# Early-fusion transformer block: rotated q and k summed in PSUM by identity products instead of on VectorE, and epsilons taken into the sums

## The reference

```
q, k = rmsnorm(q), rmsnorm(k)                    # over 16 channels, x * rsqrt(mean(x*x) + RMS_EPS)
rot(x) = concat(x1*c + x2*s, -x1*s + x2*c)       # q and k, 2 x 16 sub-heads, halves of 8
attn = softmax(causal(q k^T / sqrt(16)))         # 16 sub-heads
out = (attn[even] - lam * attn[odd]) @ v         # 8 heads, 32 wide
out = layernorm(out, eps 1e-5) * (1 - LAMBDA_INIT)
h = h + out @ Wproj^T
```

## Time and the profile before

| what | value |
| --- | --- |
| median of 3 runs | 659.81 us (658.97 to 660.0) |
| the profiled execution's own time | 662.52 us |
| its span, first to last instruction | 660.8 us |
| mean granted TensorE clock | 0.948 |
| TensorE matmuls busy | 576.4 us (87%) |
| VectorE busy | 554.1 us (84%) |
| ScalarE busy | 322.1 us (49%) |
| GpSimd busy | 309.8 us (47%) |

### The profile page before, as it was taken

How to read it: one execution, slowest core, us unless ns; L and a number is a source line. 1 busy time by engine, 2 the same in 40 slices (tenths; PEclk the granted TensorE clock), 3 DMA queues, 4 the chain that set the end, 5 groups by cost and what they waited for, 6 DMA issues and landing times. The chain is left out here.

```text
span 660.8 us, 14226 instructions
## 1 busy us (share of the span) xinstructions
PE 576.4 (87%) x3666; PEld 470.0 (71%) x3666; DVE 554.1 (84%) x1444; ACT 322.1 (49%) x760; POOL 309.8 (47%) x455
## 2 busy tenths in 40 slices
PE   5665568999999999999999998589999999999996
PEld 4554455767776776777677676478888888888885
DVE  5999847898889889888988985498888888888884
ACT  2242215655665665566565564244544444445442
POOL 2455523555455445545554553155455445545542
PEclk9878776999999999999999997789999999999999
DMA  6900000011111111111111101111111111111111
GB/s 173 325 17 23 24 16 18 27 38 41 30 40 35 35 35 38 40 34 37 35 41 29 42 23 46 30 39 49 48 54 52 54 48 54 49 48 48 57 32 35
DMA packets 33734, 31.99 MB, mean 48 GB/s; under 512 B 6098, under 2 KB 32050, under 8 KB 33714
## 3 DMA queue, kind: packets, MB, share of 16 engines
q1 hardware_dynamic: 33714, 31.75, 16.3%
HBM read 23.02 MB, written 8.71 MB: 48 GB/s over the span
## 5 line engine op out<-in xcount | busy, mean ns | idle before, releaser
L741 PE MATMUL bank<-v_sb,pt 113*113 113x33 f32 x1024 | 109.1, 262 | 0.0
L741 PEld LDWEIGHTS bank<-v_sb,pt 113*113 113x113 f32 x1024 | 108.4, 181 | 0.7 <-issue 0.7
L858 POOL TENSOR_SCALAR_AFFINE_SELECT pt<-pt 113x452 f32<-113x452 f32 x128 | 73.9, 600 | 68.5 <-ACT pt L798 68.5
L798 ACT ACTIVATE pt<-bank 113x452 f32<-113x452 f32 x128 | 63.1, 545 | 38.2 <-PE bank L729 38.2
L138 PE MATMUL bank<-wgu_hi,fx_hi 128*128 128x512 f32 x174 | 69.5, 399 | 8.0 <-DVE fx_lo L1131 8.0
L1177 POOL TENSOR_TENSOR h_deq<-fh,fhb 128x704 f32<-128x704 f32 x29 | 40.3, 1389 | 68.8 <-DVE fhb L1084 56.3
L729 PE MATMUL bank<-q_blk,k_t 64*113 64x452 f32 x256 | 67.7, 605 | 0.0
L138 PE MATMUL bank<-wgu_hi,fx_lo 128*128 128x512 f32 x174 | 66.8, 384 | 0.0
L138 PE MATMUL bank<-wgu_lo,fx_hi 128*128 128x512 f32 x174 | 66.7, 384 | 0.0
L138 PE MATMUL bank<-wqkv_hi,xo_hi 128*113 128x256 f32 (+1 forms) x128 | 50.3, 393 | 17.7 <-DVE xo_lo L923 17.7
L1191 POOL TENSOR_TENSOR fh<-fh,fhb 128x704 f32<-128x704 f32 x29 | 40.3, 1391 | 42.2 <-DVE fhb L1145 42.2
(11 more groups left out here) (160 smaller groups left out, 1531.3 us busy)
## 6 DMA issues: line engine op xcount, KB each, us to landing
xb<-h_dram SPq DMA_DIRECT2D x29, 129.0 KB, 2.1
rb<-h_dram SPq DMA_DIRECT2D x29, 128.0 KB, 2.0
h_dram<-h SPq DMA_DIRECT2D x32, 112.9 KB
out<-res SPq DMA_DIRECT2D x28, 128.0 KB, 1.7
px<-in_patches SPq DMA_DIRECT2D x9, 384.0 KB, 10.1
hx<-in_txt SPq DMA_DIRECT2D x32, 77.0 KB
hr<-in_txt SPq DMA_DIRECT2D x32, 77.0 KB
wf<-in_wgu SPq DMA_DIRECT2D x1, 1408.0 KB, 8.0
```

The source lines that it names most:

```text
L741: mm = pe.matmul(pv_ps[s % 2][0:T, s // 2, :], pt[0:T, s, :], v_sb[0:T, s // 2, :], start=True, stop=True, skip_group_check=True)
L798: act.activation(pt[0:T, GS * g:GS * (g + 1), :].rearrange("p s t -> p (s t)"), sc_ps[g % 2][0:T, :], ACT.Exp, scale=1.0 / math.sqrt(HD)). ...
L858: pool.affine_select(out=grp, in_=grp, compare_op=ALU.is_ge, fill=0.0, base=0, pattern=[[0, GS], [1, T]], channel_multiplier=-1).then_inc( ...
```

## The change

The VectorE instruction that adds the cosine and sine parts is gone, with its tile qkr. TensorE now makes the transposed sum: for each of the four chunks of 128 columns it multiplies the cosine part by the identity and then the sine part by the identity into the same PSUM block. These are ordinary float32 products and no transposes. TensorE waits for both parts, and VectorE and GpSimd wait for TensorE before they overwrite a part.

The epsilons go into the sums. The constant column beside v is sqrt(32 * 1e-5) instead of 1, w1 has a zero in this column, and the difference z is 33 columns a head instead of 32; squared with the scale 1/sqrt(32) and summed, it gives variance and epsilon at once. The squares of q and k are scaled by 1/sqrt(16) and stand beside a column that holds RMS_EPS. So four small VectorE instructions fall away (L932, L936, L951, L960), and the roots on ScalarE wait for the sums themselves.

```
             def qk_transposes(b):
-                pe.wait_ge(m["qk_roped"], b + 2)
+                pe.wait_ge(m["qk_cos"], b + 2)
+                pe.wait_ge(m["qk_sin"], 2 * b + 4)
                 after(pe, m["q_blocked"], b + 1)
                 for c in range(4):
-                    mm = pe.transpose(qkt_ps[:, c, :], qkr[0:T, c * P:(c + 1) * P], ident[0:T, 0:T])
+                    pe.matmul(qkt_ps[:, c, :], qkc[0:T, c * P:(c + 1) * P], ident[0:T, 0:T], start=True, stop=False)
+                    mm = pe.matmul(qkt_ps[:, c, :], qks[0:T, c * P:(c + 1) * P], ident[0:T, 0:T], start=False, stop=True)
                 mm.then_inc(m["qkt_made"], 1)
...
             def squares(b):
-                act.activation(sq[0:T, :], qk_ps[0:T, :], ACT.Square).then_inc(m["qk_squared"], 1)
+                act.activation(sq[0:T, :, 0:HD], blocks(qk_ps[0:T, :], HD), ACT.Square,
+                               scale=1.0 / math.sqrt(HD)).then_inc(m["qk_squared"], 1)
...
             def z_square(b):
-                act.activation(z2[0:T, :], z[0:T, :], ACT.Square).then_inc(m["z_squared"], 1)
+                act.activation(z2[0:T], z[0:T], ACT.Square, scale=1.0 / math.sqrt(VD)).then_inc(m["z_squared"], 1)
...
             def sines(b):
-                after(pool, m["qk_roped"], b + 1)
+                after(pool, m["qkt_made"], b + 1)
...
         def attention_vector(dve):
-            dve.memset(v_sb[:, :, VD:VD + 1], 1.0).then_inc(m["ones_set"], 1)
+            dve.memset(v_sb[:, :, VD:VD + 1], SUM_COLUMN).then_inc(m["ones_set"], 1)
+            dve.memset(sq[:, :, HD:HD + 1], RMS_EPS).then_inc(m["ones_set"], 1)
+            dve.memset(w1[:, :, VD:VD + 1], 0.0).then_inc(m["ones_set"], 1)
...
             def cosines(b):
                 dve.wait_ge(m["qk_scaled"], b + 2)
+                after(dve, m["qkt_made"], b + 1)
...
-            def rope_sum(b):
-                dve.wait_ge(m["qk_cos"], b + 2)
-                dve.wait_ge(m["qk_sin"], 2 * b + 4)
-                after(dve, m["qkt_made"], b + 1)
-                dve.tensor_tensor(qkr[0:T, :], qkc[0:T, :], qks[0:T, :], ALU.add).then_inc(m["qk_roped"], 1)
...
-                dve.tensor_copy(s0[0:T, :], pv_ps[0][0:T, :, VD]).then_inc(m["mix_step"], 1)
-                dve.scalar_tensor_tensor(ratio[0:T, :], s0[0:T, :], lam[0:T, :], rs_1[0:T, :], ALU.mult,
+                dve.scalar_tensor_tensor(ratio[0:T, :], pv_ps[0][0:T, :, VD], lam[0:T, :], rs_1[0:T, :], ALU.mult,
                                          ALU.mult).then_inc(m["mix_step"], 1)
-                dve.scalar_tensor_tensor(eps0[0:T, :], s0[0:T, :], LN_EPS, s0[0:T, :], ALU.mult,
-                                         ALU.mult).then_inc(m["z_sums"], 1)
...
-                dve.tensor_tensor(blocks(z[0:T, :], VD), pv_ps[0][0:T, :, 0:VD], blocks(w1[0:T, :], VD),
-                                  ALU.subtract).then_inc(m["mix_step"], 1)
+                dve.tensor_tensor(z[0:T], pv_ps[0][0:T], w1[0:T], ALU.subtract).then_inc(m["mix_step"], 1)
...
-                dve.tensor_reduce(ssz[0:T, :], blocks(z2[0:T, :], VD), AXX, ALU.add).then_inc(m["z_sums"], 1)
-            def z_var(b):
-                dve.wait_ge(m["z_sums"], 2 * b)
-                dve.scalar_tensor_tensor(var[0:T, HEADS], ssz[0:T, :], 1.0 / VD, eps0[0:T, :], ALU.mult,
-                                         ALU.add).then_inc(m["z_var"], 1)
+                dve.tensor_reduce(var[0:T, HEADS], z2[0:T], AXX, ALU.add).then_inc(m["z_sums"], 1)
...
-                dve.tensor_reduce(ssq[0:T, :], blocks(sq[0:T, :], HD), AXX, ALU.add).then_inc(m["qk_sums"], 1)
-            def qk_var(b):
-                dve.wait_ge(m["qk_sums"], b + 3)
-                dve.tensor_scalar(var[0:T, QK], ssq[0:T, :], 1.0 / HD, RMS_EPS, ALU.mult, ALU.add).then_inc(m["qk_var"], 1)
+                dve.tensor_reduce(var[0:T, QK], sq[0:T], AXX, ALU.add).then_inc(m["qk_sums"], 1)
...
-                    (3, ln_sums), (-1, mix), (1, rope_sum), (-2, residual),
-                    (2, qk_sums), (-1, z_sums), (-2, out_sums), (-1, z_var), (2, qk_var),
+                    (3, ln_sums), (-1, mix), (-2, residual),
+                    (2, qk_sums), (-1, z_sums), (-2, out_sums),
```

More of the change, by code:

```diff
@@ L65 @@
 RMS_EPS = float(np.finfo(np.float32).eps)
+SUM_COLUMN = math.sqrt(VD * LN_EPS)
 LAMBDA_INIT = 0.8 - 0.6 * math.exp(-0.3 * 4)
@@ L168, in early_fusion @@
         xo_hi, xo_lo = sb("xo_hi", [P, 2 * KD, T], F32R), sb("xo_lo", [P, 2 * KD, T], F32R)
-        sq = sb("sq", [P, 2 * D])
-        ssq = sb("ssq", [P, 2 * SH])
+        sq = sb("sq", [P, 2 * SH, HD + 1])
         NV = 2 + NH + 2 * SH
@@ L176, in early_fusion @@
         st_in, st_out = sb("st_in", [P, 6]), sb("st_out", [P, 6])
-        qkn, qkc, qks, qkr = (sb(f"rope_{i}", [P, 2 * D]) for i in range(4))
+        qkn, qkc, qks = (sb(f"rope_{i}", [P, 2 * D]) for i in range(3))
         k_t = sb("k_t", [P, KD, T])
@@ L182, in early_fusion @@
         pt = sb("pt", [P, SH, T])
-        s0, rs_1, ratio, eps0, ssz = (sb(f"sum_{i}", [P, NH]) for i in range(5))
-        w1, z, z2, o = (sb(f"mix_{i}", [P, D]) for i in range(4))
+        rs_1, ratio = (sb(f"sum_{i}", [P, NH]) for i in range(2))
+        w1, z, z2 = (sb(f"mix_{i}", [P, NH, VD + 1]) for i in range(3))
+        o = sb("mix_o", [P, D])
         h2 = sb("h2", [P, HX])
@@ L195, in early_fusion @@
         names = ("hx_loaded hr_loaded h2_stored ln_stats out_stats variances root_log root_made newton ln_applied "
-                 "xo_made xo_high xo_low qk_made v_made qk_squared qk_sums qk_var "
-                 "qk_scaled qk_cos qk_sin qk_roped qkt_made kt_copied q_blocked v_staged v_moved scores_made "
-                 "exp_made masked pv_made mix_step z_sums z_squared z_var o_made proj_made h2_added h2_ready ones_set")
+                 "xo_made xo_high xo_low qk_made v_made qk_squared qk_sums "
+                 "qk_scaled qk_cos qk_sin qkt_made kt_copied q_blocked v_staged v_moved scores_made "
+                 "exp_made masked pv_made mix_step z_sums z_squared o_made proj_made h2_added h2_ready ones_set")
         m = {n: sem("a_" + n) for n in names.split()}
@@ L737, in pv @@
                     pe.wait_ge(m["v_moved"], b + 1)
-                    after(pe, m["mix_step"], 5 * b)
+                    after(pe, m["mix_step"], 4 * b)
                 pe.wait_ge(m["masked"], NG * b + g + 1)
@@ L774, in roots @@
                 if seq(b, 2):
-                    act.wait_ge(m["qk_var"], b + 3)
+                    act.wait_ge(m["qk_sums"], b + 3)
                 if seq(b, -1):
-                    act.wait_ge(m["z_var"], b)
+                    act.wait_ge(m["z_sums"], b)
                 act.activation(root[0:T], var[0:T], ACT.Ln).then_inc(m["root_log"], 1)
@@ L817, in z_square @@
             def z_square(b):
-                act.wait_ge(m["mix_step"], 5 * b)
-                act.activation(z2[0:T, :], z[0:T, :], ACT.Square).then_inc(m["z_squared"], 1)
+                act.wait_ge(m["mix_step"], 4 * b)
+                act.activation(z2[0:T], z[0:T], ACT.Square, scale=1.0 / math.sqrt(VD)).then_inc(m["z_squared"], 1)
             def steps(b, between=None):
@@ L864, in v_move @@
                 if isinstance(b, int) and b == -1:
-                    pool.wait_ge(m["ones_set"], 3)
+                    pool.wait_ge(m["ones_set"], 5)
                 pass_wait(pool, pool_passed)
@@ L879, in attention_vector @@
         def attention_vector(dve):
-            dve.memset(v_sb[:, :, VD:VD + 1], 1.0).then_inc(m["ones_set"], 1)
+            dve.memset(v_sb[:, :, VD:VD + 1], SUM_COLUMN).then_inc(m["ones_set"], 1)
+            dve.memset(sq[:, :, HD:HD + 1], RMS_EPS).then_inc(m["ones_set"], 1)
+            dve.memset(w1[:, :, VD:VD + 1], 0.0).then_inc(m["ones_set"], 1)
             dve.memset(var[:], 1.0).then_inc(m["ones_set"], 1)
             dve.memset(moments[:], 1.0).then_inc(m["ones_set"], 1)
-            dve.wait_ge(m["ones_set"], 3)
+            dve.wait_ge(m["ones_set"], 5)
             def newton_step(b):
@@ L899, in o_apply @@
             def o_apply(b):
-                dve.scalar_tensor_tensor(blocks(o[0:T, :], VD), blocks(z[0:T, :], VD), 1.0 - LAMBDA_INIT,
+                dve.scalar_tensor_tensor(blocks(o[0:T, :], VD), z[0:T, :, 0:VD], 1.0 - LAMBDA_INIT,
                                          spread(rstd[0:T, HEADS], VD), ALU.mult, ALU.mult).then_inc(m["o_made"], 1)
@@ L931, in mix @@
                 dve.reciprocal(rs_1[0:T, :], pv_ps[1][0:T, :, VD]).then_inc(m["mix_step"], 1)
-                dve.tensor_copy(s0[0:T, :], pv_ps[0][0:T, :, VD]).then_inc(m["mix_step"], 1)
-                dve.wait_ge(m["mix_step"], 5 * b - 3)
-                dve.scalar_tensor_tensor(ratio[0:T, :], s0[0:T, :], lam[0:T, :], rs_1[0:T, :], ALU.mult,
+                dve.wait_ge(m["mix_step"], 4 * b - 3)
+                dve.scalar_tensor_tensor(ratio[0:T, :], pv_ps[0][0:T, :, VD], lam[0:T, :], rs_1[0:T, :], ALU.mult,
@@ L935, in mix @@
```

(13 more changed lines are left out.)

## The result

The changed kernel takes 702.74 us (median, 702.39 to 703.39), the kernel before, on the same chip, 659.39 us. The ratio is 1.0661, 95% interval 1.0642 to 1.0679: 6.6% slower. The prediction was 699 us, with a range of 678 to 709. The profiled executions are 662.52 and 702.39 us, a difference of 39.9, for which the prediction's sum said 39.2; their mean granted clocks were 0.948 and 0.956, which matters for the ends of the attention, as told further down.

What follows compares the result with a forecast made beforehand. TensorE was taken as the bound, VectorE close behind. 39.6 us (30 steps of +1.32) + 0.5 + 0.6 - 1.5 gives +39.2, profiled 662.5 to 701.7; against the 659.8 median, 699 us, range 678 to 709.

Steps and rivals of the forecast that it cites:

- TensorE is the bound: Attention step: TensorE's round of 9.58 us sets the pace, VectorE close behind.
- The idle weight load is no wait for rope_sum: Weight load of the q and k transposes: its 0.67 us idle waited for the array, so TensorE has no slack there.
- The rival at 679 us: Weight load of the q and k transposes truly waits for rope_sum: 0.67 us a step returns, +19.5 us; chance 0.07.
- the faster one: TensorE's waits of 0.58 and 0.67 us are VectorE's lateness: 1.25 us a step returns, 654 us; chance 0.04.
- the 0.58 us before the q and k product: TensorE's wait there follows ScalarE's copy and VectorE's low half; a freer VectorE was counted to shorten it by nothing.
- Sixteen instructions at 0.11: TensorE's q and k part: eight float32 products as sixteen instructions, 1.76 us in place of 0.44, +1.32 a step.
- Four transposes for one product: Rival for TensorE's q and k part: a product costs four transposes, +3.08 us a step, 752 us; chance 0.04.
- One instruction for a product: Rival for TensorE's q and k part: eight instructions for four, +0.44 us a step, 673 us; chance 0.06.
- Nothing else in the step moves: Step's other waits: sine and cosine parts cost nothing, and the late copy of k nothing, with 1.4 us to spare.
- VectorE's 1.6 us a step: VectorE's removed sum and four small instructions: 1.6 us a step, worth nothing while TensorE stays full.
- The ends: Attention steps outside the full ones: step -1 +0.5 us, step 30 +0.6, steps 31 to 33 together -1.5.
- VectorE's slack of 0.5 us: Normalised rows end at 314.56, TensorE takes them up at 315.05: about 0.5 us of slack on VectorE's side.

Runs made afterwards that it cites:

- eps_late_pv: Last four pv products moved behind the next step's transposes, against the kernel with the epsilon edit alone; 654.48 us, ratio 0.9912 to the kernel before.
- before_late_pv: Only the last four pv products moved behind the next step's transposes, against the kernel before; 679.21 us, ratio 1.0308.
- eps_only: Epsilons inside the sums, but q and k summed on VectorE and transposed as before, against the kernel before; 660.1 us, ratio 0.9995.

## Why the prediction held, point by point

*TensorE is the bound.* Shown: taking an eighth of VectorE's busy time away (89.3 to 77.6 us of 100) left the step at 9.6 us, and an unused VectorE sum in the changed kernel cost nothing.

*The idle weight load is no wait for rope_sum.* Shown by the trace after: that load is again idle for 0.67 us, with no rope_sum in the kernel, and is put down to "issue". The rival at 679 us falls, and with it the faster one, which needed these 0.67 us. The other half of the faster rival, the 0.58 us before the q and k product, is unchanged too.

*Sixteen instructions at 0.11.* The count was right. The price was 1.88 / 16 = 0.1175; this is the term that was mis-sized. Behind the first product, which takes 0.31 us (328.76 to 329.07), the products stand 0.223 us apart, 0.112 an instruction, and the first one's start adds 0.09 that the sum left out. The row that the price came from was a mixture as well. Of the four transposes, the first takes 0.15 us (310.80 to 310.95 in the step of the earlier trace rows) and the other three stand 0.097 apart:

```profile
310.95 0.45 PE L756 MATMUL bank_b<-ident,rope 113*128 113x113 f32 x3
```

So an instruction of a product is not of the transpose's pace but somewhat slower, 0.112 for 0.097, and that 0.11 came so near to it is luck. The part grew by 1.44 us and not 1.32. Over 28 steps this makes the 3.1 us between the 37.0 that these steps would have had at 1.32 and the 40.1 measured.

*Four transposes for one product.* Falls: a product costs two instructions. By the Trainium skill, "TensorE: Matmul & The Clock Gate", section "Terms", transpose mode is 4 times faster for float32; here four float32 products took 0.98 us and four transposes 0.44, a factor of 2.2, and the measurement decides.

*One instruction for a product* holds for float32r alone (676.09 us, near that rival's 673) and not for the float32 of the change.

*Nothing else in the step moves.* Right for the sine part's wait, the late copy of k (1.0 us of idle time ahead of it, TensorE unharmed) and the roots.

*VectorE's 1.6 us a step* was too much, though with TensorE as the bound nothing hung on it. Busy time in total fell from 554.1 to 515.0 us, by 39 and not by some 50. The idle time came out as said: 1.22 + 1.08 + 0.89 = 3.2 us in the step.

*The ends.* I gave steps -1 and 0 together +1.8 and what lies behind step 29 +0.4 (1.32 + 0.6 - 1.5). Against the profiled execution of the kernel before they measure +0.3 and -0.6. But that execution had a mean granted clock of 0.948, and the changed kernel's one of 0.956. In the later series the kernel before took 659.0 to 660.9 us where its clock was 0.956, and 662.0 to 664.2 where it was 0.948. The kernel with the epsilon edit alone was profiled at 0.956 (659.87 us). Its transposes of q and k in steps 1 and 29:

```profile
117.42 0.61 PE L757 MATMUL bank_b<-ident,rope 113*128 113x113 f32 x4
...
385.53 0.60 PE L757 MATMUL bank_b<-ident,rope 113*128 113x113 f32 x4
```

Clock ahead of step 1, the kernel before first and then this one:

```profile
100.00:119.28 19.28, 17.18 (x84) 10.83 (x85) 14.20 (x40) 11.05 (x31) 9.25 (x14) 0.73 0.08 25
100.00:119.28 19.28, 17.52 (x103) 11.52 (x102) 14.11 (x36) 11.56 (x33) 10.05 (x16) 0.82 0.09 26
```

Against this kernel the changed one is +2.2 us up to step 1, +40.1 between steps 1 and 29, and +0.3 behind: the ends together are +2.5, forecast +2.2. One step of their reasoning was wrong: the sixteen instructions of step -1 ran from 97.78 to 99.7 at full clock and not at half, and were done before the old four began (101.12).

So 39.9 for 39.2 is luck: the lower clock of the profiled execution of before hid about 3 us, as much as the mis-sized term adds. On the medians the rise is 43.3 us, 4.1 more than the sum, and 3.6 of these are the term's 0.12 in 30 steps. The 699 us, counted from the median, came out 3.7 us low for this reason.

*VectorE's slack of 0.5 us* was misread, though nothing in the forecast hung on it. It was slack only in the handover of the normalised rows. With the last pv products late, the kernel before got slower and not a little faster, even in the steps without a stretch of lower clock (9.73 us on average), and with the epsilon edit only 0.2 us of the step could be won.

## What to carry to other kernels

Before work is moved from one nearly full engine to another, find whose round sets the step: lay the distances between starts over one step and look for the engine whose parts add up without waits. Count a float32 product with the identity as two instructions, each with its weight load, where a float32 transpose is one. And when an order is changed to fill a wait, expect the next chain close behind; here it stood at 9.4 us, 0.2 behind TensorE's 9.6. Compare the ends of two profiles only at like granted clock: here 0.948 for 0.956 was worth about 3 us.

## What the runs showed of the hardware

The clock was not steady in the kernels that moved pv. In stretches in which TensorE was as busy as before or busier, the granted clock fell for some microseconds towards the lower of its two levels, 1.2 GHz for 2.4. Two windows of 50 us from eps_late_pv's profiled execution, with the mean clock in the column behind the five engines:

```profile
150.00:200.00 50.00, 49.05 (x333) 37.44 (x332) 40.07 (x106) 28.98 (x75) 24.36 (x45) 0.93 0.12 35
200.00:250.00 50.00, 49.06 (x347) 37.43 (x347) 42.45 (x113) 30.78 (x79) 26.41 (x50) 1.00 0.14 38
```

TensorE was busy 49 of 50 us in both. That execution took 661.96 us, the other four 653.5 to 654.7. In before_late_pv the mean from 210 to 310 us was 0.96. The kernel before held 1.00 there. What makes it fall I did not find. What it costs can be read: in eps_late_pv two steps between steps 1 and 29 take 12.43 and 12.48 us where their neighbours take 9.40, 3 us each. Two steps of before_late_pv, the first with such a stretch and the second without:

```profile
157.31:169.91 12.60, 12.21 (x67) 9.14 (x67) 8.47 (x27) 5.64 (x15) 4.89 (x9) 0.73 0.10 28
169.91:179.69 9.78, 9.27 (x68) 7.10 (x66) 8.47 (x25) 6.07 (x16) 4.47 (x9) 1.00 0.13 36
```

VectorE's instructions on eight elements a row vary in length with what GpSimd does beside them. The epsilon product (L936, 0.62 us on average in the loop) lasted 0.15 or 0.16 us in five of 32 steps; in the other 27 it lasted about 0.6 us or more, and in all 27 it ended within 0.03 us of a GpSimd instruction that ran beside it. The ratio in before_late_pv (L941, 0.82 us from 248.49 to 249.31) ended with the sine part, at 249.29:

```profile
247.87 1.42 POOL L857 TENSOR_TENSOR rope<-rope,trig 113x256 f32<-113x256 f32 x2
```

The row variances of eps_only (L983) ended so in all 25 steps in which they lasted 0.55 us. So a small instruction's length there is mostly a wait, and when one is taken away the next can take the wait over. No run changed GpSimd's work alone to test this.
